# Gated cross-attention and expert block on one core: a rebuilt first stage, turned x and k kept in SBUF, one ScalarE table

## What is computed

```
q = layernorm(x)
ig, fg = [q, k, v] @ gate_w.T + gate_b            # 8 + 8 gates per token
cs = cumsum(log_sigmoid(fg));  a = ig - cs
m = running max of a;  D = tril(exp(a[t] - m[s]))  # log_D with its row maximum taken out
C = (q k^T / sqrt(32)) * D
h = C v / (max(|sum C|, exp(-(cs + m))) + 1e-6)
x = x + tanh(g0) * layernorm(h) * ln_scale
x = x + tanh(g1) * top-2 experts of layernorm(x)   # silu(x w1) * (x w3) @ w2
```

## Time and profile before

| | |
|---|---|
| median of 3 runs | 1065.64 us (1060.14 to 1067.1) |
| profiled execution | 1068.61 us; its span 1066.3 us |
| busy in the span | PE 847.0 (79%), DVE 634.1 (59%), ACT 424.3 (40%), POOL 393.4 (37%) |
| mean granted TensorE clock | 0.806 |
| moved by DMA | 187.79 MB, 176 GB/s over the span |
| chain that ended last | PE 36%, DMA 7%, DVE 5% of the span; its pieces start at 467.7 us |

### The profile page before, as it was taken

The page is one execution under the profiler, slowest core; times in us unless marked ns, Lnnn a source line. Parts: engine busy times, 40 slices in busy tenths (PEclk is TensorE's granted clock), DMA queues, the critical chain, the costliest instruction groups (busy, mean ns, idle before and its releaser), DMA issues.

```text
span 1066.3 us, 19701 instructions
## 1 busy us (share of the span) xinstructions
PE 847.0 (79%) x5990; PEld 642.0 (60%) x5990; DVE 634.1 (59%) x1715; ACT 424.3 (40%) x960; POOL 393.4 (37%) x403
## 2 busy tenths in 40 slices
PE   5994976958577877753267999989898999989895
PEld 5993343524334443432166778878686878878784
DVE  5223599596877869594794555545454545545452
ACT  3222665556464646452001434433332433433341
POOL 1000456354443626262002244434534344433533
PEclk9999975567575656565555999999898999999998
...
GB/s 165 195 117 31 155 236 174 152 200 133 207 101 223 122 186 166 147 152 87 31 167 31 137 242 231 242 232 210 237 232 247 196 248 208 238 223 206 255 225 56
DMA packets 90796, 187.79 MB, mean 176 GB/s; under 512 B 14176, under 2 KB 51552, under 8 KB 90720
## 3 DMA queue, kind: packets, MB, share of 16 engines
...
HBM read 145.10 MB, written 42.73 MB: 176 GB/s over the span
## 4 chain that ended last, share of the span: by engine, by line
PE 36%; DMA 7%; DVE 5%; issue 4%; POOL 2%; ACT 1%; SPq 1%; DVEq 0%; POOLq 0%; ACTq 0%
PE bank L997 32%; DMA w<-w_d 6%; PE bank L907 3%; PE bank L991 1%; POOL out L979 1%; DVE xl L1051 1%; DMA out<-res,sid 1%; DVE topi L806 0%; SPq L946 0%; PE bank L759 0%; DVE hlo L1084 0%; DMA w_d<-whl 0%; POOL xg L969 0%; DVE hf L1097 0%; ACT hh L1062 0%
## 5 line engine op out<-in xcount | busy, mean ns | idle before, releaser
L997 PE MATMUL bank<-xh,w 128*128 128x256 bf16 (+1 forms) x1760 | 282.6, 271 | 27.8 <-DMA w<-w_d 16.0
L997 PE MATMUL bank<-xl,w 128*128 128x256 bf16 (+1 forms) x880 | 229.3, 270 | 0.0
L997 PEld LDWEIGHTS bank<-xh,w 128*128 128x128 bf16 x1760 | 170.1, 101 | 58.6 <-issue 27.4
L1068 ACT ACTIVATE sg<-bank 128x256 f32<-128x256 f32 (+1 forms) x240 | 86.6, 361 | 284.4 <-PE bank L997 284.4
L1095 DVE TENSOR_TENSOR hf<-sg,bank 128x256 f32<-128x256 f32 (+1 forms) x200 | 78.8, 394 | 152.2 <-ACT sg L1068 151.8
L979 POOL DMA_INDIRECT out<-res,sid x72 | 116.7, 1621 | 120.5 <-DVE res L1109 88.1
L997 PE MATMUL bank<-w,hh 128*128 128x256 bf16 (+1 forms) x864 | 150.1, 273 | 0.0
L591 POOL TENSOR_TENSOR whl<-wst,whl 128x1224 bf16<-128x1224 f32 x32 | 83.4, 2605 | 138.8 <-ACT whl L561 138.8
L487 PE MATMUL bank<-qbd,kvb 128*128 128x512 f32 x128 | 110.3, 958 | 11.7 <-DVE Cm L600 10.6
L997 PE MATMUL bank<-w,hlo 128*128 128x256 bf16 (+1 forms) x432 | 117.5, 272 | 0.0
L1084 DVE TENSOR_TENSOR hlo<-hf,hh 128x256 bf16<-128x256 f32 (+1 forms) x240 | 93.7, 390 | 5.6 <-ACT hh L1062 1.3
...
## 6 DMA issues: line engine op xcount, KB each, us to landing
...
```

Of the source, the lines that this page charges most:

```text
L997: mm = nc.tensor.matmul(dst, l, r, start=(n == 0), stop=(n == len(pairs) - 1))
L1068: nc.scalar.activation(sg[m % 2][0:K, 0:N], bank[0:K, 2 + (NM * w + m) % 4, 0:N], ACT.Silu).then_inc(f_sg, 1)
```

## The change

x and turned k of all eight batches are loaded into buffers of their own, with no wait, and the turned x and k stay in SBUF for the attention (`qT`, `kT`); `qT_d` and its stores and loads are gone, and the attention loads v alone. The gate weights become the stationary operand: `wwin` holds, between zeros, 8 forget columns and 8 input columns 64 apart, and a window of 128 columns that starts at 64 - 8n puts batch n's gates on its rows; all batches add up in one bank (`GATES`), with 512 tokens as the moving columns: four float32 products a batch. A one-row product adds the biases. The glue reads that bank. ScalarE loads one table that holds both Ln and Exp, and the loops of the attention are written out for all engines (batches 2 to 6). GpSimd splits a, VectorE splits -m, and each part is stored when ready. TensorE does the first scores ahead of the decay products. The attention's buffers share space with those of the router and the experts, so the router waits for the weight stores.

The diff, cut to its core; the removed bodies of `a_x_sync` to `a_pe` stand in the kernel above. The same replacement of `with ... Fori(2, NB - 1)` by `for b in range(2, NB - 1)` stands in all five programs, and `kvb`, `qtb` become `vb`, `kT`, `qT` wherever they are read.

```diff
-        qT_d = dram("qT_d", [NT, P, D], F32)
...
-        wg = sb("wg", [P, 6, 2 * NH]); wgkv = sb("wgkv", [P, 2, 2 * NH]); ifb_s = sb("ifb_s", [BH, 2])
+        wg = sb("wg", [P, 6, 2 * NH]); wwin = sb("wwin", [P, 4, 3 * BH]); fib_s = sb("fib_s", [1, P])
...
+        qT = attn("qT", [P, NB, NC, D]); kT = attn("kT", [P, NB, NC, D])
+        vb = [attn(f"vb{c}", [P, NH * DV]) for c in range(NC)]
...
+        xa = [early(f"xa{n}", [P, NC, D]) for n in range(NB)]
+        qn = [(hl, y)[u // NC][:, u % NC, :] for u in range(8)]
...
+            nc.gpsimd.memset(wwin[:, :, :], 0.0).then_inc(s_wz, 1)
...
-        def wgkv_dve(dve):
+        def wwin_dve(dve):
             dve.wait_ge(s_small, 16 * 6)
-            nc.vector.tensor_tensor(wgkv[:, :, :], wg[:, 2:4, :], wg[:, 4:6, :], ALU.add).then_inc(s_wgkv, 1)
+            dve.wait_ge(s_wz, 1)
+            for n, i in enumerate((1, 0)):
+                dst = wwin[:, :, BH * (n + 1):BH * (n + 1) + NH]
+                gate = wg[:, :, i * NH:(i + 1) * NH]
+                nc.vector.tensor_copy(dst[:, 0:2, :], gate[:, 0:2, :]).then_inc(s_wwin, 1)
+                nc.vector.tensor_tensor(dst[:, 2:4, :], gate[:, 2:4, :], gate[:, 4:6, :], ALU.add).then_inc(s_wwin, 1)
...
+        def a_x_sync(sp, n):
+            sp.dma_start(xa[n][:, :, :], x_v[:, n * NC:(n + 1) * NC, :]).then_inc(a_x[n], 16)
+
+        def a_k_sync(sp, n):
+            sp.dma_start(kT[:, n, :, :], k_v[:, n * NC:(n + 1) * NC, 0:D]).then_inc(a_k[n], 16)
+
+        def a_stats_dve(dve, n):
+            ge(dve, a_x[n], 16)
+            for c in range(NC):
+                nc.vector.bn_stats(stA[:, n * NC + c, :], xa[n][:, c, :]).then_inc(a_st, 1)
+            ge(dve, a_st, n * NC + NC)
+            for c in range(NC):
+                nc.vector.bn_aggr(mvA[:, n * NC + c, :], stA[:, n * NC + c, :]).then_inc(a_mv, 1)
+
+        def a_qn_dve(dve, n):
+            ge(dve, a_rs, n + 1)
+            ge(dve, a_tr, n * 2 - 2)
+            for c in range(NC):
+                t = n * NC + c
+                nc.vector.tensor_scalar(qn[(n % 2) * NC + c][:, :], xa[n][:, c, :], mvA[:, t, 0:1], rsA[:, t:t + 1],
+                                        ALU.subtract, ALU.mult).then_inc(a_q, 1)
+
+        def a_norm_act(act, n):
+            ts = slice(n * NC, (n + 1) * NC)
+            ge(act, a_mv, n * NC + NC)
+            nc.scalar.activation(lvA[:, ts], mvA[:, ts, 1], ACT.Ln, bias=eps_c[:, 0:1]).then_inc(a_lv, 1)
+            ge(act, a_lv, n + 1)
+            nc.scalar.activation(rsA[:, ts], lvA[:, ts], ACT.Exp, scale=-0.5).then_inc(a_rs, 1)
+
+        def a_qt_act(act, n):
+            for v in range(2):
+                ge(act, a_tr, n * 2 + (v + 1))
+                nc.scalar.copy(qT[:, n, 2 * v:2 * v + 2, :].rearrange("p c d -> p (c d)"),
+                               bank[:, 2 * (n % 2) + v, :]).then_inc(a_qt, 1)
+
+        GATES = bank[:, 4, :]
+
+        def a_pe_bias(pe):
+            pe.wait_ge(s_small, 16 * 6)
+            nc.tensor.matmul(GATES, fib_s[0:1, :], ones_row[0:1, :], start=True, stop=False)
+
+        def a_pe_gates(pe, n):
+
+            o = BH - n * NH
+            ge(pe, a_k[n], 16)
+            for k in range(KD):
+                nc.tensor.matmul(GATES, wwin[:, KD + k, o:o + P], kT[:, n, :, k * P:(k + 1) * P], start=False, stop=False)
+            ge(pe, a_qt, n * 2 + 2)
+            for k in range(KD):
+                mm = nc.tensor.matmul(GATES, wwin[:, k, o:o + P], qT[:, n, :, k * P:(k + 1) * P], start=False,
+                                      stop=(n == NB - 1 and k == KD - 1))
             mm.then_inc(a_gp, 1)
 
+        def a_pe_turn(pe, n):
+            for v in range(2):
+                ge(pe, a_q, n * NC + (2 * v + 2))
+                ge(pe, a_qt, n * 2 + (v - 3))
                 for j in range(2):
                     for k in range(KD):
+                        mm = nc.tensor.transpose(bank[:, 2 * (n % 2) + v, (2 * j + k) * P:(2 * j + k + 1) * P],
+                                                 qn[(n % 2) * NC + 2 * v + j][:, k * P:(k + 1) * P], identf[:, :])
                 mm.then_inc(a_tr, 1)
...
         def g_actf_all(act):
-            act.wait_ge(g_tp, 1)
-            nc.scalar.activation(z[:, :], bank[0:BH, 5, :], ACT.Identity, bias=ifb_s[:, 1:2]).then_inc(g_act, 1)
-            act.wait_ge(g_dve, 1)
-            nc.scalar.activation(g2[:, :], g1[:, :], ACT.Exp).then_inc(g_act, 1)
+            act.wait_ge(a_gp, NB)
+            nc.scalar.activation(g1[:, :], GATES[0:BH, :], ACT.Abs).then_inc(g_act, 1)
+            act.wait_ge(g_act, 1)
+            nc.scalar.activation(g2[:, :], g1[:, :], ACT.Exp, scale=-1.0).then_inc(g_act, 1)
             act.wait_ge(g_act, 2)
             nc.scalar.activation(g3[:, :], g2[:, :], ACT.Ln, bias=one_c[0:BH, 0:1]).then_inc(g_act, 1)
-            act.wait_ge(g_dve, 11)
+            act.wait_ge(g_dve, 14)
             nc.scalar.activation(gw[:, :], g1[:, :], ACT.Exp).then_inc(g_act, 1)
             nc.scalar.activation(gE[:, :], g2[:, :], ACT.Exp).then_inc(g_act, 1)
             nc.scalar.activation(gn[:, :], g3[:, :], ACT.Exp, scale=-1.0).then_inc(g_act, 1)
             nc.scalar.activation(gdx[:, :], gd[:, :], ACT.Exp).then_inc(g_act, 1)
...
         def g_pe_all(pe):
-            pe.wait_ge(a_gs, NT // 2)
-            for k in range(2):
-                for c in range(NC):
-                    mm = nc.tensor.transpose(bank[0:BH, 4 + k, c * P:(c + 1) * P],
-                                             gall[:, c, k, :, :].rearrange("p b h -> p (b h)"), identf[:, :])
-            mm.then_inc(g_tp, 1)
             pe.wait_ge(g_act, 7)
-            pe.wait_ge(g_spread, 1)
             for k, src in enumerate((gw, gE, gn)):
                 for c in range(NC):
-                    mm = nc.tensor.transpose(bank[:, (6, 7, 2)[k], c * BH:(c + 1) * BH], src[:, c * P:(c + 1) * P],
+                    mm = nc.tensor.transpose(bank[:, 5 + k, c * BH:(c + 1) * BH], src[:, c * P:(c + 1) * P],
                                              identf[0:BH, 0:BH])
             mm.then_inc(g_col, 1)
+            b_scores_pe(pe, 0, 0)
+            pe.wait_ge(g_spread, 1)
             for n in range(2 * NB):
-                mm = nc.tensor.matmul(bank[:, 3, n * NC:(n + 1) * NC], spread[:, n * P:(n + 1) * P], gdx[:, :], start=True, stop=True)
+                mm = nc.tensor.matmul(bank[:, 4, n * NC:(n + 1) * NC], spread[:, n * P:(n + 1) * P], gdx[:, :], start=True, stop=True)
             mm.then_inc(g_dec, 1)
             pe.wait_ge(g_cols, 4)
...
             V.tensor_copy(spread[:, :].rearrange("p (b d) -> p b d", d=DH),
                           identf[0:BH, 0:BH].unsqueeze(2).to_broadcast([BH, BH, DH])).then_inc(g_spread, 1)
-            dve.wait_ge(g_act, 1)
-
-            V.scalar_tensor_tensor(g1[:, :], z[:, :], -1.0, z[:, :], ALU.mult, ALU.min).then_inc(g_dve, 1)
             dve.wait_ge(g_act, 3)
 
-            V.scalar_tensor_tensor(lf[:, :], z[:, :], 0.0, g3[:, :], ALU.min, ALU.subtract).then_inc(g_dve, 1)
+            V.scalar_tensor_tensor(lf[:, :], GATES[0:BH, :], 0.0, g3[:, :], ALU.min, ALU.subtract).then_inc(g_dve, 1)
+            dve.wait_ge(g_dve, 1)
+            V.tensor_tensor_scan(cs[:, :], ones_row[0:BH, :], lf[:, :], 0.0, ALU.mult, ALU.add).then_inc(g_dve, 1)
             dve.wait_ge(g_dve, 2)
-            V.tensor_tensor_scan(cs[:, :], ones_row[0:BH, :], lf[:, :], 0.0, ALU.mult, ALU.add).then_inc(g_dve, 1)
+            V.tensor_tensor(ga[:, :], GATES[BH:2 * BH, :], cs[:, :], ALU.subtract).then_inc(g_dve, 1)
             dve.wait_ge(g_dve, 3)
-            V.scalar_tensor_tensor(ga[:, :], bank[0:BH, 4, :], ifb_s[:, 0:1], cs[:, :], ALU.add,
-                                   ALU.subtract).then_inc(g_dve, 1)
+            V.tensor_tensor_scan(gm[:, :], ga[:, :], ga[:, :], -3e38, ALU.max, ALU.max).then_inc(g_dve, 1)
             dve.wait_ge(g_dve, 4)
-            V.tensor_tensor_scan(gm[:, :], ga[:, :], ga[:, :], -3e38, ALU.max, ALU.max).then_inc(g_dve, 1)
-            dve.wait_ge(g_dve, 5)
             c4 = lambda t: t[:, :].rearrange("p (c s) -> p c s", c=NC)
             m_end = ends(gm)
+            me = c4(gm)[:, :, P - 1]
+
+            V.tensor_scalar(mp[0][:, :], gm[:, :], -1.0, None, ALU.mult).then_inc(g_dve, 1)
+            dve.wait_ge(g_dve, 5)
+            V.scalar_tensor_tensor(r2[:, :], gm[:, :], -1.0, mp[0][:, :], ALU.mult, ALU.subtract).then_inc(g_dve, 1)
+            V.memset(gd[:, 0:1], 0.0).then_inc(g_dve, 1)
+            dve.wait_ge(g_dve, 6)
+            V.tensor_copy(mp[1][:, :], r2[:, :]).then_inc(g_dve, 1)
+            V.tensor_tensor(gd[:, 1:NC], me[:, 0:NC - 1], me[:, 1:NC], ALU.subtract).then_inc(g_dve, 1)
+            dve.wait_ge(g_dve, 8)
+            V.tensor_tensor(mp[2][:, :], r2[:, :], mp[1][:, :], ALU.subtract).then_inc(g_dve, 1)
...
+        def g_pool(pool):
+
+            G = nc.gpsimd
+            pool.wait_ge(g_dve, 3)
+            G.tensor_copy(ap[0][:, :], ga[:, :]).then_inc(g_pl, 1)
```

(58 more changed lines are left out.)

195 lines of the change are left out of this document (48 added, 147 removed).

## The result

The changed kernel takes **1018.84 us** (median of 4 runs, 1018.52 to 1030.57) against 1066.37 for the kernel before, measured with it: ratio 0.959, 95% interval 0.951 to 0.967. I had forecast 1025 (1012 to 1047). The profiled execution took 1018.94 us, its span 1017.1.

The account below looks back on a forecast made before the run. TensorE at 1.2 GHz was taken to bound the first stage, no engine being full in the attention. 1068.6 - 29.0 (start to first state product) - 8.8 - 2.9 (tables) = 1027.9, against the median 1025 us; range 1012 to 1047.

Parts of the forecast that it names:

- T: First stage: time at which the last gate product ends, claimed 55.0 us against 81.2 before; sign 52 to 58.
- S: Start of the first state product, after the glue: claimed at 92.4 us instead of 121.4, so -29.0 us.
- The clock: First stage: TensorE rises from 1.2 to 2.4 GHz in batch 0's gates, taking 6.1 us (bounds 3.8 and 7.5).
- Rival 1: First stage: TensorE's clock stays low, last gate product at 87 us (or 82), time 1052 to 1057; chance 0.09.
- The unheld loads cost and give nothing: First stage: loading x and k without waits was put at 0, since DMA needs 3.3 us a batch, TensorE 4.7.
- The glue: Between last gate product and first state product: 37.4 us instead of 40.2, 2.8 shorter, with 1.5 for held VectorE steps.
- Scores ahead buys little: Glue: scores before decay products gain little, since TensorE must do both (6.8 and 6.9 us) before chunk 1.
- Tables: One ScalarE table: attention -8.8 us (7 x 1.25, through GpSimd's subtraction and y), last layer norms -2.9 us.
- "Free" straight-line code: Attention: Python loops for hardware loops put at 0, from batch 1 straight-line 50.1 us, the next, looped, 49.7.
- Rivals 2 (batches keep 49.7): Attention keeps its 49.7 us a batch, as y meets another GpSimd step or wait: 1034 us; chance 0.10.
- 3 (tables not taken): Rival on ScalarE's tables: Ln and Exp still load in turn, about 1038 us; chance 0.04.
- Rival 4: Attention: ScalarE's earlier casts put GpSimd's weight subtraction onto VectorE's Cl, up to 2.3 us a chunk, 1098 us; chance 0.05.

Follow-up runs that it names:

- experiment 1: Changed kernel with its gate products turned back to 128 small ones of 16 gate columns, loads still unheld and one table: 1050.99 us.
- experiment 2: Changed kernel with each gate product of 512 columns split into four of 128, same stationary weights: 1017.48 us.
- experiment 3: Changed kernel with its first-stage loads of x and k held again at the distance of two buffers: 1037.03 us.
- experiments 8 and 9: Changed kernel; 8: GpSimd's chunk 2 weight subtraction held until y is written, chunk 2's weight store moved behind turned y's copies, 1001.78 us; 9: store moved only, 1023.21 us.
- experiment 5: Changed kernel with the 32 decay products back ahead of the first chunk's scores: 1022.81 us.

## Why the prediction held, and where it did not

**The sum.** To R the change gained 48.0 us; I had 40.7. Of the difference of 7.3, 6.5 is in T, 48.5 instead of 55.0 and outside the 52 to 58 that I had given as its sign. From T to S I was 0.2 off, from S to R 0.6 (12.3 for 11.7).

**The clock: right.** It rose in the first batch of gates, experiment 1 shows that all the rest together moves the stage by 1.7 us, and experiment 2 that the new layout at the old clock would gain nothing. Rival 1 is out.

**T: mis-sized by 6.5.** The gates start at 15.1 us (I had 16.2). The rise comes sooner, within the first of the two product groups, which I had bounded by the 3.3 us run before the rise in the earlier trace rows and then taken near the slow end: the first batch takes 3.9 us instead of 6.1, 2 us. And a product is 0.86 us, not the 0.96 of the earlier trace rows, since between equal products the hand-over vanishes; I had allowed for that in rival 1 and not in the forecast. With the shorter gaps it gives 3.3 us.

**"The unheld loads cost and give nothing": wrong, and the total hid it.** Held loads cost 16.4 us (experiment 3). I divided bytes by rate (3.3 us a batch, below TensorE's 4.7) and never asked how long one load takes from issue to landing when VectorE stands behind it. T came out near because the loads in fact are unheld: that this term did no harm was luck, not reading. The stage's gain is no sum of parts: unheld loads (with all else but the products) give 1.7 (81.2 to 79.5), the turned products alone 16.3 (to 64.9), both 32.7. In the kernel before, SyncE's 42.8 us of waits were covered by a slow TensorE; at twice the pace the cover is gone.

**The glue: right in sum, S at T + 37.2 for 37.4, with errors inside that cancelled, which is luck.** VectorE was held 2.6 us by GpSimd, where I took 1.5 and the Trainium skill's rule ("SBUF — State Buffer", "Who interferes with whom") gave 3.9. The trace agrees that steps with two SBUF inputs are held (1.52 us for 0.68). I had excepted the casts, which the same section of the Trainium skill does not: it lists copies, casts and tensor_scalar steps, the form of y, among those that can contend. Two casts were longer (0.65 and 0.71 us instead of 0.41), and y, my row for the two-input rule, has one SBUF tensor only and was held all the same (3.05 us for four, 1.37 freed). Moving the split of a to GpSimd was a loss of 0.7 us, which I had not priced as a whole. I had the scores wait for the written rows, until T + 15.1 and 1.5 more, with the transposes done at T + 13.8. In the trace the first scores start at T + 15.7, right behind the last transposes (63.62, then 64.19), without a wait: the exponentials' path, longer by the held steps, had become as late as the rows. The rows are hardly earlier: with decays early and VectorE's split together TensorE waits 0.15 us for them there. And ScalarE's exponentials stood behind the copy of the decays (78.11), 0.9 us of wait for TensorE. "Scores ahead buys little" held (experiment 5); that the decays could have run in TensorE's idle 14 us I did not ask.

**Tables: right in mechanism and nearly in size**, 8.6 from N1 to N8 for 8.8. It is y behind GpSimd's subtraction; experiments 8 and 9 show that this is what the batch hangs on. Of the 2.9 for the last layer norms, 1.3 show between N8 and R; the other bare load of the earlier trace rows (492.54) stands ahead of N8 and lies in the 1.8 of the last interval. Together the tables are worth 9.8 (8.6 and 1.3, rounded) where I had 11.7, so that the 12.3 from S to R are near my sum only because the loops' 2.5, which I had at 0, came on top. By the Trainium skill ("ScalarE: Activation LUTs", "What ACT_TABLE_LOAD costs") 2.66 us a switch would have given about twice these terms; the trace disagrees, the activation follows its load at once (292.07 to 293.36).

**"Free" straight-line code: wrong by 2.5 us.** I compared batch 1, straight-line, with batch 2, looped; but a first batch differs in more than its loop. In the changed kernel, where every batch is straight-line, N1 to the next norm product is 48.5 us and then 48.0 a batch. That comparison hid the loops' 0.5 us a batch.

Rivals 2 (batches keep 49.7) and 3 (tables not taken) did not come. Rival 4 neither: VectorE's Cl takes 1207 ns on average, 1204 before.
